# A four-layer graph network on Trainium2: the node update with W4 and its activations as fp16 halves, and a new order of each engine's step

## The reference

```python
h = mish(edge_feat @ W1 + b1)
messages = mish(h @ W2 + b2)
agg = jax.ops.segment_sum(messages, dst, num_segments=x.shape[0])
u = mish(jnp.concatenate([x, agg], axis=-1) @ W3 + b3)
out = u @ W4 + b4
y = x + out
mu = jnp.mean(y, axis=-1, keepdims=True)
var = jnp.mean(jnp.square(y - mu), axis=-1, keepdims=True)
return (y - mu) * jax.lax.rsqrt(var + LN_EPS) * gamma + beta
```

## Time and profile before

| | us |
|---|---|
| median of 3 runs | 3074.97 (3073.33 to 3088.87) |
| the profiled execution's own time | 3073.27 |
| its span, first to last instruction | 3071.0 |
| PE busy | 2573.3 (84%) |
| DVE busy | 1851.7 (60%) |
| ACT busy | 1505.4 (49%) |
| POOL busy | 1221.5 (40%) |

### The profile page before, as it was taken

The page is one execution under the profiler, slowest core; times in us unless marked ns, Lnnn a source line. Parts: engine busy times, 40 slices in busy tenths (PEclk is TensorE's granted clock), DMA queues, the critical chain, the costliest instruction groups (busy, mean ns, idle before and its releaser), DMA issues. The chain is left out here.

```text
span 3071.0 us, 44367 instructions
## 1 busy us (share of the span) xinstructions
PE 2573.3 (84%) x13170; PEld 1453.0 (47%) x13170; DVE 1851.7 (60%) x4344; ACT 1505.4 (49%) x2128; POOL 1221.5 (40%) x2065
## 2 busy tenths in 40 slices
PE   0347888789887999798979969799999999899964
PEld 0234554344443445344544547565555555444443
DVE  8744876578666876799864435345555566423333
ACT  7235665345333533355335756466666666332270
POOL 3666874236332332365545511133333333100146
PEclk9999998899998999899989989899999999999976
DMA  5154442278766887666553322322222234101268
GB/s 173 59 213 124 150 145 92 78 184 201 134 123 156 203 171 152 192 221 220 181 182 105 101 80 85 103 81 95 96 99 102 89 134 138 71 1 38 57 225 312
DMA packets 379160, 412.03 MB, mean 134 GB/s; under 512 B 198351, under 2 KB 237683, under 8 KB 376316
## 3 DMA queue, kind: packets, MB, share of 16 engines
q1 hardware_dynamic: 350364, 335.34, 37.0%
q0 software_dynamic: 28640, 74.78, 8.1%
HBM read 171.50 MB, written 197.28 MB: 120 GB/s over the span
## 5 line engine op out<-in xcount | busy, mean ns | idle before, releaser
L215 PE MATMUL s_ps_z<-s_w,slots 128*128 128x512 f16 x2844 | 645.7, 384 | 41.7 <-DMA s_bias<-in_L_gnn_b 41.7
L215 PEld LDWEIGHTS s_ps_z<-s_w,slots 128*128 128x128 f16 (+1 forms) x2844 | 280.9, 99 | 363.3 <-DMA s_bias<-in_L_gnn_b 43.1
L1571 ACT ACTIVATE s_g<-s_g,s_rn 128x512 f32<-128x512 f32 x237 | 170.0, 717 | 287.7 <-POOL s_rn L1461 287.7
L2239 PE MATMUL u_ps_o<-u_w,u_uT 128*128 128x512 f32 x632 | 288.6, 599 | 0.2 <-DVE u_uT L2110 0.2
L1461 POOL TENSOR_TENSOR s_rn<-s_em,minus_half 128x1 f32<-128x1 f32 x237 | 179.6, 758 | 253.0 <-DVE s_em L1515 245.1
L1500 DVE SCALAR_TENSOR_TENSOR s_g<-s_ps_z,s_f,s_bias 128x512 f32<-128x512 f32 x237 | 177.9, 751 | 140.3 <-PE s_ps_z L215 132.0
L2221 PE MATMUL u_ps_z<-slots,u_w 128*128 (+2 forms) x1920 | 236.7, 273 | 0.0
L2349 PE MATMUL z_ps_z<-slots,z_w 128*128 128x512 f16 (+1 forms) x960 | 211.7, 380 | 7.2 <-DMA z_w<-split_root 7.2
L2221 PEld LDWEIGHTS u_ps_z<-slots,u_w 128*128 128x128 f16 x1920 | 173.9, 98 | 37.7 <-issue 0.4
L716 DVE BATCH_NORM_STATS2 u_ny_st<-u_ps_o 128x6 f32<-128x512 f32 x79 | 54.7, 692 | 213.7 <-PE u_ps_o L2239 213.7
L743 ACT ACTIVATE u_h<-u_x,u_n_sh,u_n_rs 128x512 f32<-128x512 f32 x79 | 64.3, 814 | 229.3 <-POOL u_n_sh L738 229.3
...
...
## 6 DMA issues: line engine op xcount, KB each, us to landing
...
```

Of the source, the lines that this page charges most:

```text
L215: ins = nc.tensor.matmul(out_ap, a(c), w[:, part * size + c * n:part * size + (c + 1) * n], start=first and c == 0 and m == 0, stop=stop a ...
L1571: nc.scalar.activation(g[b][:, :], g[b][:, :], ACT.Relu, scale=rn[v.buf(2)][:, 0:1]).then_inc(s_h, 1)
L2239: ins = nc.tensor.matmul(ps_o[b][:, :], ut_tile(v, c), w4[:, c * D:(c + 1) * D], start=False, stop=c == C - 1)
```

## The change

In `node_update()`, W4 becomes a unit (fp16 halves from DRAM), and so does u: it is scaled by a power of two, `g`, and split by ACT into `u_hi` (`hi_u`) and by DVE into `u_lo` (`lo_u`). The fp32 matmuls of `second` become eight fp16 ones with `u_hi` and four with `u_lo`. `u_uT`, `u_hi` and `u_lo` have one buffer each, where `u_uT` had two. The bias b3 leaves PE: ACT's sigmoid takes it as its bias operand and DVE's `times_z` adds it, each as one column of a chunk, so both now work by chunks of 256 columns. An explicit table load before `tanh` selects a set that holds sigmoid too. To choose `g`, `edge_messages()` records the largest magnitude of each tile of message products (`z_max`), and a string of one-column operations ahead of the first pair works it out. Its DVE loop is written out in full. Lastly the orders of the steps are new. The core of the diff:

```diff
-    units = {"conv": (Wc, 1), "edge": (W1[0:2 * D, :], 2), "update": (W3[0:D, :], 1),
+    units = {"conv": (Wc, 1), "edge": (W1[0:2 * D, :], 2), "update": (W3[0:D, :], 1), "out": (W4, 1),
              **{f"{kind}{l}": (ws[l], 1) for l in range(3) for kind, ws in (("self", Wself), ("neigh", Wneigh))},
...
+
+    def load_sigmoid_and_tanh(act):
+        act.add_instruction(mybir.InstLoadActFuncSet(name=nc.get_next_instruction_name(), act_func_set_id=SIGMOID_AND_TANH,
+                                                     engine=mybir.EngineType.Activation))
...
+                    wait_count(dve, s_zmax, v.t - 1)
                     nc.vector.tensor_scalar(out=tot[b][:, :], in0=ps_g[b][:, :], scalar1=scale[:, 0:1],
                                             scalar2=None, op0=MUL).then_inc(s_tot, 1)
+                    dve.wait_ge(s_tot, v.t + 1)
+                    nc.vector.tensor_reduce(out=z_max[:, v.t:v.t + 1], in_=tot[b][:, :], op=MAX, axis=AX.X,
+                                            apply_absolute_value=True).then_inc(s_zmax, 1)
                 pipeline(dve, ET, (0, z_sum), (0, cap), (0, lambda v: mish.poly(dve, v)), (1, add), (3, totals),
-                         (0, lambda v: mish.result(dve, r[:, :], v)), peel=8)
+                         (0, lambda v: mish.result(dve, r[:, :], v)), peel=ET, loop_end=ET)
...
-                def times_z(k):
+                def times_z(v, tiles):
+                    for c in range(C):
+                        dve.wait_ge(s_th, mish_count(v, c // 2))
+                        part = chunk(uT, c, tiles)
+                        ins = nc.vector.scalar_tensor_tensor(out=part, in0=z_chunk(v, c, tiles), scalar=b3_cols[:, c:c + 1],
+                                                             in1=part, op0=ADD, op1=MUL)
+                        if c % 2:
+                            ins.then_inc(s_u, 1)
+
+                def lo_u(k):
                     def stage(v, tiles):
-                        b = v.j // 2
-                        dve.wait_ge(s_th, mish_count(v, k))
-                        part = uT[b][:, k * D:(k + 1) * D].rearrange("p (c n) -> p c n", c=2)[:, :, 0:tiles * P]
-                        z = ps_z[b][k][:, :].rearrange("p (c n) -> p c n", c=2)[:, :, 0:tiles * P]
-                        nc.vector.tensor_tensor(out=part, in0=z, in1=part, op=MUL).then_inc(s_u, 1)
+                        dve.wait_ge(s_uhi, mish_count(v, k))
+                        nc.vector.scalar_tensor_tensor(out=half(u_lo, k, tiles), in0=half(uT, k, tiles), scalar=g[:, 0:1],
+                                                       in1=half(u_hi, k, tiles), op0=MUL, op1=SUB).then_inc(s_ulo, 1)
                     return stage
 
-                def y_stats(v):
+                def centred(v):
                     dve.wait_ge(s_mm4, v.t + 1)
...
-                def residual(v):
-                    b = v.buf(4)
                     dve.wait_ge(normy.s_mv, v.t + 1)
                     nc.vector.scalar_tensor_tensor(out=ps_o[v.buf(2)][:, :], in0=ps_o[v.buf(2)][:, :],
                                                    scalar=normy.mv[v.buf(2)][:, 0:1], in1=gam[:, :], op0=SUB,
                                                    op1=MUL).then_inc(s_yn, 1)
+
+                def residual(v):
+                    b = v.buf(4)
                     dve.wait_ge(s_yn, v.t + 1)
                     dve.wait_ge(s_ry, v.t + 1)
                     dve.wait_ge(s_xb, v.t + 1)
...
                 def step(v):
-                    of_pair(v, 2, residual, (1,))
-                    of_pair(v, 0, add_messages(0))
-                    of_pair(v, 0, add_messages(1))
-                    of_pair(v, 1, y_stats, (0,))
+                    of_pair(v, 1, centred, (0,))
+                    whole_pair(v, 0, times_z)
+                    whole_pair(v, 0, lo_u(0))
+                    whole_pair(v, 0, lo_u(1))
                     of_pair(v, 1, residual, (0,))
+                    of_pair(v, 1, centred, (1,))
+                    of_pair(v, -1, add_messages(0))
+                    of_pair(v, -1, add_messages(1))
                     of_pair(v, 2, lo)
-                    whole_pair(v, 0, times_z(0))
-                    whole_pair(v, 0, times_z(1))
-                    of_pair(v, 1, y_stats, (1,))
+                    of_pair(v, 1, residual, (1,))
                 by_pairs(dve, step)
...
-                sigmoid = each_half(s_s, z_there, ACT.Sigmoid, minus_f[:, 0:1], first=True)
-                log = each_half(s_l, s_there, ACT.Ln, 1.0, bias=floor_col[:, 0:1])
-                tanh = each_half(s_th, l_there, ACT.Tanh, -1.0)
+                def sigmoid(k):
+                    def stage(v, tiles):
+                        z_there(v, k)
+                        wait_count(act, s_ulo, mish_count(v, k) - 2)
+                        for c in (2 * k, 2 * k + 1):
+                            ins = nc.scalar.activation(chunk(uT, c, tiles), z_chunk(v, c, tiles), ACT.Sigmoid,
+                                                       scale=minus_f[:, 0:1], bias=minus_b3[:, c:c + 1])
+                        ins.then_inc(s_s, 1)
+                    return stage
+
+                def log(v, tiles):
+                    for k in range(2):
+                        act.wait_ge(s_s, mish_count(v, k))
+                        nc.scalar.activation(half(uT, k, tiles), half(uT, k, tiles), ACT.Ln, scale=1.0,
+                                             bias=floor_col[:, 0:1]).then_inc(s_l, 1)
+
+                def tanh(v, tiles):
+                    load_sigmoid_and_tanh(act)
+                    for k in range(2):
+                        act.wait_ge(s_l, mish_count(v, k))
+                        nc.scalar.activation(half(uT, k, tiles), half(uT, k, tiles), ACT.Tanh, scale=-1.0).then_inc(s_th, 1)
+
+                def hi_u(v, tiles):
+                    wait_count(act, s_mm4, v.t)
+                    for k in range(2):
+                        act.wait_ge(s_u, mish_count(v, k))
+                        nc.scalar.activation(half(u_hi, k, tiles), half(uT, k, tiles), ACT.Copy,
+                                             scale=g[:, 0:1]).then_inc(s_uhi, 1)
 
                 def next_rows(v):
...
                 def step(v):
-                    of_pair(v, 2, next_rows)
-                    whole_pair(v, 0, sigmoid)
+                    whole_pair(v, 0, sigmoid(0))
+                    of_pair(v, 2, next_rows, (0,))
+                    whole_pair(v, 0, sigmoid(1))
                     whole_pair(v, 0, log)
+                    whole_pair(v, 0, tanh)
+                    of_pair(v, 2, next_rows, (1,))
+                    whole_pair(v, 0, hi_u)
                     of_pair(v, 2, hi)
-                    whole_pair(v, 0, tanh)
                 by_pairs(act, step)
 
...
-                    b = v.j // 2
                     wait_count(pe, s_u, 2 * v.g - 2)
                     pair_slots = slots16[:, bass.ds(v.t * 2 * D, tiles * 2 * D)].rearrange("p (t x) -> p t x", t=tiles)
                     for c in range(C):
-                        z = ps_z[b][c // 2][:, (c % 2) * 2 * P:(c % 2) * 2 * P + tiles * P]
-                        nc.tensor.matmul(z, b3_rows[:, c * P:(c + 1) * P], ones3[:, 0:tiles * P], start=True, stop=False)
+                        z = z_chunk(v, c, tiles)
                         for k in range(C):
                             for m, (part, wpart) in enumerate(((0, 0), (1, 0), (0, 1))):
                                 at = wpart * cols["update"] + k * D + c * P
                                 ins = nc.tensor.matmul(z, w3[:, at:at + P],
                                                        pair_slots[:, :, part * D + k * P:part * D + (k + 1) * P],
-                                                       start=False, stop=k == C - 1 and m == 2)
+                                                       start=k == 0 and m == 0, stop=k == C - 1 and m == 2)
...
-                    pe.wait_ge(s_w4, 1)
+                    pe.wait_ge(s_g, 1)
+                    nc.tensor.matmul(ps_o[b][:, :], ones3[:, :], b4_rows[:, :], start=True, stop=False)
                     for part in range(2):
                         for c in range(C):
                             nc.tensor.matmul(ps_o[b][:, c * P:(c + 1) * P],
                                              slots16[:, bass.ds(v.t * 2 * D + part * D + c * P, P)],
                                              unscale[:, :], start=False, stop=False)
-                    pe.wait_ge(s_u, 2 * v.g + 2)
+                    pe.wait_ge(s_uhi, 2 * v.g + 2)
+                    for part in range(2):
+                        for c in range(C):
+                            nc.tensor.matmul(ps_o[b][:, :], chunk_of_tile(u_hi, v, c),
+                                             w4[:, part * cols["out"] + c * D:part * cols["out"] + (c + 1) * D],
+                                             start=False, stop=False)
+                    pe.wait_ge(s_ulo, 2 * v.g + 2)
```

(26 more changed lines are left out.)

137 lines of the change are left out of this document (83 added, 54 removed).

## The result

The changed kernel takes 2993.03 us (median of 4 runs, 2990.66 to 3002.35) against 3076.84 (4 runs, 3073.33 to 3088.87) for the kernel before on the same chip: a ratio of 0.9727, 95% interval 0.9693 to 0.976. On a second chip it was 0.9702 (0.9688 to 0.9715). The forecast was 2987 us, a ratio of 0.971.

The account below looks back on a forecast made before the run. PE, busy throughout the 16.10 us steps, was taken to bound the kernel. From the profiled 3073.3 us, -96 + 4.6 + 1 + 3 = -87.4 gave 2985.9, as a median 2987; 8-in-10 range 2955 to 3032.

Parts of the forecast that it names:

- PE's sum: Node update: PE's own work in a step, predicted to fall from 16.10 to 12.96 us, taken as 13.0.
- the zone: Node update, pairs 29 to 39: 10 steps predicted to gain 1.2 us each, 12 us together.
- the rings: Node update: dependence chains from one pair's second sigmoid to the next's, 13.0 us through PE, 12.6 through DVE and POOL.
- The zone's ring: Pairs 29 to 39: chain through residual, centred of tile 1, message additions and the next pair's first sigmoid, 14.9 us a step.
- The number of steps: Node update: of 39.5 steps, 29 outside the zone gain 2.9 us each and 10 in it 1.2, together 96 us.
- Run-in and run-out: Node update's start and end: the first second waits for u of pair 0; +3 us with the run-out.
- `prepare()`: One more unit of 2048 columns there puts a DVE reduction and the low half on the path: +4.6 us.
- Edge messages: A new DVE reduction of 0.6 us a tile, nearly covered by DVE's wait for PE: +1 us (0 to 6).
- PE alone: Rival for the node update: PE sets every step, in the zone too, with shorter rings; 2963 us, chance 0.2.
- longer rings: Rival for the node update: steps of 14.3 us outside the zone and 15.7 in it; 3027 us, chance 0.22.
- two loads are seen, not three: Rival on ACT: the saved table load doesn't vanish, rings through tanh grow by 1.3 us; 3032 us, chance 0.02.
- The clock rival: Node update: PE's waits lower its clock; at 0.75 a step takes 17.3 us, slower at 3131 us, chance 0.03.

Follow-up runs that it names:

- The extra load: The changed kernel with one more table load in each pair's step, just before the one ahead of tanh; 3022.99 us.
- the early `centred`: The changed kernel with DVE's centred of tile 1 moved directly behind times_z, ahead of lo_u and residual of tile 0; 3014.67 us.
- the old order: The changed kernel, halves kept, with all four engines' steps in the order of the kernel before; ratio 0.9984 to the kernel before.

## Why the prediction was right

The forecast was the right one, and so was its mechanism: PE's sum outside the zone, a ring in it. By its own steps:

- PE's step: 12.96 worked out, 13.03 measured; PE busy for 100% and 92%, where I had said over 97% and about 87%. The gain outside the zone is 3.07 us a step; I had taken 2.9, to allow for jitter between two rings and PE. There is none: each step is 13.03. The extra load and the early `centred` show the rings at about 12.9, as near as I had counted them (12.6 and 13.0).
- The zone's ring: 14.9 worked out, 14.46 measured. Its parts in the timeline above, counted as in the prediction: second sigmoid to `times_z` 5.63 (predicted 5.60; 2457.22 to 2462.85), `times_z` to `residual` 3.17 (3.03), `residual` 1.61 (1.75), `centred` 1.59 (1.83), the first addition 0.83 (0.76), sigmoid and `next_rows` 1.62 (1.88). Three pieces that I had taken to the end of an instruction are shorter: the next one on the same engine starts about 0.1 us before that end. In `centred` a wait of 0.15 us inside the tile that I had read it from is missing as well.
- The number of steps: I counted 29 outside and 10 in the zone; of the steps that were 16.10 only 36 can gain. 29 x 2.9 + 10 x 1.2 = 96 and the measured 96.2 agree so well by luck, because the count was too high and the gain of a step too low.
- Run-in and run-out: +3 predicted, -0.9 measured. The string of one-column operations now stands partly behind PE's first matmul, which waits for the last constants, but the first pair's `update` covers it.
- `prepare()`: +4.6 predicted, 4.6 measured on the second chip.
- Edge messages and what else: the stretches between `prepare()` and the node update, code that the change leaves as it is but for the edge messages, are longer by 3.2, 1.0 and 1.2 us and shorter by 2.0 on the second chip, and the last stage longer by 2.5. The first of these scatters from 417.7 to 423.0 us between kernels with the same code there. The 1.2 is the edge messages' own stage: 187.0 to 188.5 us in the twelve profiles with the new reduction, 186.9 and 187.2 in the two without. So +1 fits, and the upper bound of 6 does not.
- The sum: -87.4 predicted; the two pairs of profiles give -79.5 and -86.7 of span. The first holds 7.8 us of `prepare()` in place of 4.6, by the waits named above, and 5.5 us in the unchanged last stage.
- The rivals: PE alone (2963) fails in the zone, longer rings (3027) fail everywhere, two loads are seen, not three. The clock rival did not happen here: with waits of 1.20 us a step the clock stays at 1.00. But its mechanism is real, as the kernels with waits of about 2 us and more show. I had given it the right condition, the waits of PE, and only part of the price: 13.0 / c leaves out the waits themselves. With PE's order alone changed back, the mean clock over the steps is 0.85; 13.03 / 0.85 = 15.3, and with waits of 3.6 to 3.8 us that is about 19, where 19.3 was measured. It also holds only where PE is in the ring, as the old order shows.

The prediction did not say how much of the gain hangs on the order. The halves and b3 off PE gain 0.2% with the old order (12.6 us of the node update, part of which `prepare()` takes back); the new order with fp32 W4, and b3 off PE, gains 48.8 us of the node update's 97.2. Which share of it the order has by itself, with b3 left on PE, wasn't tried.
